# Fused double attention on one core: three maxima ahead of both score pairs in every step, two loads of A's keys moved, batch 0's maxima spread

## The reference

```python
# x: (8, 1024, 256) = (batch, token, channel)
xn = (x - mean) / sqrt(var + 1e-5)                  # over the channels
out = x + A(xn) + B(xn)

def A(h):       # latent attention: 8 heads, d_k 128, latent 32, rotary part 32
    c_q, c_kv = h @ W_DQ + b_DQ, h @ W_DKV + b_DKV  # 32 wide
    q = concat(c_q @ W_UQ + b_UQ, c_q @ W_QR + b_QR)            # 128 + 32 a head
    k = concat(c_kv @ W_UK + b_UK, h @ W_KR + b_KR)             # the 32 are shared
    v = c_kv @ W_UV + b_UV
    return softmax(q k^T / sqrt(160)) v, heads joined, @ W_O + b_O

def B(h):       # 16 heads of 16 dims, REG = 5 register tokens
    q, k, v = h @ W_qkv
    sim = mean over heads of cosine(q[5:], g_info), scaled to 0..1
    pos = sim > 0.9
    masked(m) = softmax(q k^T / 4 over registers and the tokens of m) v
    registers: (masked(pos) + masked(~pos)) / 2
    token: masked(pos) if pos[token] else masked(~pos)
    return all @ W_proj + b_proj
```

## Time and profile before

| | us |
|---|---|
| median of three runs | 2925.47 |
| lowest and highest | 2915.63, 2926.33 |
| the profiled execution, whole | 2916.49 |
| its span, from the first instruction to the last | 2914.7 |
| pass, in the profiled execution | 395.1 |
| A phases: batch 0, then the others | 127.8, 138.3 to 140.0 |
| B phases of batches 0 to 7 | 173.9, 180.2, 174.2, 178.7, 174.6, 177.8, 174.3, 160.3 |
| mean granted TensorE clock, 1 is full speed | 0.988 |

### The profile page before, as it was taken

One profiled execution on the slowest core, in us unless ns is written; L12 is line 12 of the kernel. 1 busy time (PEld: TensorE's weight loads), 2 busy tenths in 40 slices (PEclk: granted clock), 3 DMA queues, 4 the chain that ended last, 5 costly groups with the idle time before them and its releaser, 6 DMA issues.

```text
span 2914.7 us, 45214 instructions
## 1 busy us (share of the span) xinstructions
PE 2778.8 (95%) x16834; PEld 1264.0 (43%) x16834; DVE 2203.8 (76%) x4048; ACT 1761.9 (60%) x2143; POOL 1187.5 (41%) x424
## 2 busy tenths in 40 slices
PE   7899989999999999999999999999999999999997
PEld 5555534434443444444433444344434444344432
DVE  4566638788887788778878888878877887888880
ACT  3444445775467645775467646864577547754684
POOL 3323249214850088016721385118701672148411
PEclk9999989999999999999999999999999999999999
DMA  5855464234212520234122421352023412342001
GB/s 190 259 215 187 166 175 78 51 63 77 54 30 61 95 54 26 69 60 70 40 51 62 75 57 30 68 90 60 20 67 62 70 40 51 70 76 50 21 18 38
DMA packets 132636, 225.51 MB, mean 77 GB/s; under 512 B 52642, under 2 KB 83266, under 8 KB 130224
## 3 DMA queue, kind: packets, MB, share of 16 engines
q1 hardware_dynamic: 132416, 222.62, 31.4%
HBM read 143.70 MB, written 78.59 MB: 76 GB/s over the span
## 4 chain that ended last, share of the span: by engine, by line
PE 72%; DVE 21%; ACT 3%; issue 2%; DMA 1%; POOL 1%; SPq 0%; POOLq 0%; ACTq 0%; DVEq 0%
PE O L1266 21%; DVE mx L1538 17%; PE M L1178 15%; PE S L1248 7%; PE M L1172 7%; PE S L1245 7%; PE M L1224 2%; PE M L1132 2%; PE M L1226 2%; PE M L1215 2%; PE M L1150 1%; PE M L1191 1%; PE M L1146 1%; ACT PT L1019 1%; DVE QB L1519 1%
## 5 line engine op out<-in xcount | busy, mean ns | idle before, releaser
L1538 DVE TENSOR_REDUCE mx<-M 128x1 f32<-128x512 f32 x3037 | 1899.6, 681 | 389.4 <-PE M L1178 266.3
L1019 ACT ACTIVATE PTx<-S 128x1024 f32<-128x1024 f32 x768 | 744.4, 1022 | 461.3 <-PE S L1245 286.6
L1019 ACT ACTIVATE PT<-S 128x1024 f32<-128x1024 f32 x768 | 745.0, 1023 | 311.8 <-PE S L1245 151.1
L1178 PE MATMUL M<-KB,QB 50*128 50x512 f32 x2048 | 660.8, 479 | 33.5 <-DVE mx L1538 10.2
L889 POOL TENSOR_TENSOR SUM<-SUM,PTx 128x2048 f32<-128x2048 f32 x128 | 585.2, 4572 | 27.2 <-POOL SUM L889 22.2
L1178 PEld LDWEIGHTS M<-KB,QB 50*128 50x128 f32 x2048 | 278.8, 184 | 618.0 <-DVE mx L1538 316.5
L1248 PE MATMUL S<-QB,KB 52*128 52x512 f32 x2048 | 439.9, 427 | 4.0 <-ACT PT L1019 2.2
L1172 PE MATMUL M<-KA,QA 98*128 98x512 f32 x989 | 371.0, 446 | 14.6 <-DVE mx L1538 4.9
L889 POOL TENSOR_TENSOR SUM<-PT 128x2048 f32<-128x2048 f32 x64 | 292.2, 4566 | 170.7 <-ACT PT L1019 138.1
L1245 PE MATMUL S<-QA,KA 114*128 114x512 f32 (+1 forms) x1024 | 315.4, 417 | 9.6 <-ACT PT L1019 9.4
L1172 PEld LDWEIGHTS M<-KA,QA 98*128 98x128 f32 x989 | 169.5, 188 | 260.2 <-issue 120.3
(11 more groups left out here) (208 smaller groups left out, 1925.2 us busy)
## 6 DMA issues: line engine op xcount, KB each, us to landing
KA<-kt_d SPq DMA_DIRECT2D x48, 512.0 KB, 8.1
QB<-qk_d SPq DMA_DIRECT2D x192, 128.0 KB
KB<-qk_d SPq DMA_DIRECT2D x192, 128.0 KB
qk_d<-QB SPq DMA_DIRECT2D x16, 1024.0 KB, 4.2
kt_d<-QB SPq DMA_DIRECT2D x16, 1024.0 KB, 4.0
RB<-recb_d SPq DMA_DIRECT2D x64, 256.0 KB
vb_d<-VB SPq DMA_DIRECT2D x8, 1536.0 KB, 5.8
VB<-vb_d SPq DMA_DIRECT2D x8, 1536.0 KB, 9.3
```

Source lines behind the costliest of these rows:

```text
L1019: nc.scalar.activation(probs(k)[:, 2 * pair:2 * pair + 2, :], Sg[pair][:, :].rearrange("p (j s) -> p j s", j=2), ACT.Exp, scale=SCALE_A if ...
L1178: done = mm(m[:, :], QB[rows, 2 * q + a, at:at + P], KB[rows, 2 * q + a, keys], start=True, stop=True)
L1538: v.tensor_reduce(mx[:, g % 2, unit, kh:kh + 1], m[:, :], AX.X, ALU.max).then_inc(free, 1)
```

## The change

Four things change.

1. `jobs_b`: the units of every B step outside the registers' steps are laid out as (3, 0), all three ahead of the first pair, none between the pairs. Before it was (2, 1) for steps with B units; A units were (3, 0) already. A fourth unit stands behind the second pair as before.
2. `jobs_a`: the same for A steps with A units, 0 to 10, formerly (2, 1).
3. In the B phase the loads of A's keys move from steps 14 and 22 to steps 22 and 30. In the pass, the second half of batch 0's keys and its VA move out of "first" into a job "second" in batch 3.
4. Batch 0's B units, formerly at their common places in steps 10 to 31, are spread evenly over steps 6 to 31 by `first_slots`.

```diff
--- before.py
+++ after.py
@@ -39,7 +39,7 @@
 STORES = ("cq", "qk0", "kt0", "kb", "qk1", "kt1", "qk2", "qk3")
 RING = 4
 COS_PARTS = 8
-SILENT = ("x", "t", "ln", "root", "inv", "cq", "first", "cosroot", "cos", "draw")
+SILENT = ("x", "t", "ln", "root", "inv", "cq", "first", "cosroot", "cos", "draw", "second")
 PRIMED = 1
 RS_AT, RT_AT, RV_AT, RX_AT = 5, 11, 14, 19
 PO_B, PO_A = (45, 47, 53, 55), (13, 14, 15, 16)
@@ -67,7 +67,7 @@
     s += [("root", b + 1)] if more else [("cosroot", 6)]
     s += [("qk0", b, 0), ("qk0", b, 1), ("cq", b)]
     s += [("inv", b + 1)] if more else []
-    s += [("first",)] if b == 1 else []
+    s += [("first",)] if b == 1 else [("second",)] if b == 3 else []
     s += [("cosroot", b - 2)] if b in (2, 4, 6) else []
     s += [("kt0", b, 0), ("kt0", b, 1)] + (q[2:4] if more else []) + [("kb", b, 0), ("kb", b, 1)]
     s += [("va", b), ("qk1", b, 0), ("qk1", b, 1)]
@@ -134,6 +134,21 @@
 UNITS, FA = unit_slots()
 
 
+def first_slots(begin):
+
+    stream = [u for k in range(STEPS_A) for u in UNITS[k] if u[0] == "mb"]
+    units, ends, n = [[] for _ in range(STEPS_A)], [[] for _ in range(STEPS_A)], STEPS_A - begin
+    for i, u in enumerate(stream):
+        k = begin + i * n // len(stream)
+        units[k].append(u)
+        if i % (4 * NC) == 4 * NC - 1:
+            ends[k + 1].append(("fa", "b", u[1]))
+    return units, ends
+
+
+UNITS0, FA0 = first_slots(6)
+
+
 def lay(step, units, fa, sizes, behind):
 
     i, n = sizes[0], sizes[0] + sizes[1]
@@ -158,7 +173,7 @@
         units = [u for u in UNITS[STEPS_A + k] if more or u[0] == "mb"]
         fa = [j for j in FA[STEPS_A + k] if more or j[1] == "b"]
         registers = RV_AT <= k < RV_AT + NC // 2
-        sizes = (2, 0) if registers else (3, 0) if units and units[0][0] == "ma" else (2, 1)
+        sizes = (2, 0) if registers else (3, 0)
         lay(s[k], units, fa, sizes, registers)
     return s
 
@@ -172,9 +187,8 @@
         for c, at in enumerate(PO_A):
             s[at][2].append(("po", 4 + c))
     for k in range(STEPS_A):
-        units = [u for u in UNITS[k] if not first or u[0] == "mb"]
-        fa = [j for j in FA[k] if not first or j[1] == "b"]
-        sizes = (2, 1) if units and units[0][0] == "ma" else (2, 0) if k in PO_A else (3, 0)
+        units, fa = (UNITS0[k], FA0[k]) if first else (UNITS[k], FA[k])
+        sizes = (2, 0) if k in PO_A and not first else (3, 0)
         lay(s[k], units, fa, sizes, False)
     return s
 
@@ -694,11 +708,13 @@
                 wait_apart(sp, sel_in, 2 * HA * 16)
                 wait_apart(sp, zeros_in, 2 * 16)
                 wait_apart(sp, ones_out, 16)
-                for name in ("cq", "kt0", "kb", "kt1"):
+                for name in ("cq", "kt0", "kb"):
                     stored(0, name)
                 load_c(0)
                 load_a(0, 0)
                 load_kb(0)
+            elif kind == "second":
+                stored(0, "kt1")
                 load_a(0, 1)
                 wait_apart(sp, va_out[0], 16)
                 load_va(0)
@@ -738,9 +754,8 @@
 
         def a_steps(n, b, before):
             for k in range(STEPS_A):
-                for _, kind, g in FA[k]:
-                    if before or kind == "b":
-                        shift(n, kind, g, a_spot(n, b, ("fa", kind, g)))
+                for _, kind, g in FA[k] if before else FA0[k]:
+                    shift(n, kind, g, a_spot(n, b, ("fa", kind, g)))
                 if not before:
                     if k == 0:
                         for i in range(2):
@@ -802,9 +817,9 @@
                         load_c(n)
                         load_kb(n)
                         load_va(n)
-                    if k == 14:
+                    if k == 22:
                         load_a(n, 0)
-                    if k == 22:
+                    if k == 30:
                         load_a(n, 1)
                     if k > 5 * NC and k % NC == 2:
                         freed(b, k // NC - 5)
```

## The result

| | before | changed |
|---|---|---|
| median, us | 2923.01 (4 runs) | 2947.79 (4 runs) |
| lowest and highest | 2915.63, 2926.33 | 2945.22, 2952.33 |
| profiled execution: span | 2914.7 | 2944.4 |
| pass | 395.1 | 384.7 |
| A phase of batch 0 | 127.8 | 140.6 |

The ratio is 1.0095, with a 95% interval of 1.0074 to 1.0116: slower by about 25 us by the medians. The spans divide the difference of 29.7 us: the pass 10.4 shorter, batch 0's A phase 12.8 longer, the rest 27.3 longer. (The profiled execution of before was one of its faster ones, 2916.49, so the spans show some 5 us more than the medians.)

What follows compares the result with a forecast made beforehand. TensorE's order was taken as the bound, with the exponentials' loop equally long. The terms 36 - 14 - 10 - 4 gave +8 us, 2924.5; half the profiled run's distance to the median made it 2929 us, range 2890 to 2947.

Steps and rivals of the forecast that it cites:

- Part 1: B steps, three maxima ahead of the scores: first score pair and its exponential one slot later, +36 us over eight batches.
- The loop of 4.49 us for two steps: Plain B steps: the exponentials' loop has no slack, so two steps grow from 4.26 to 4.49 us.
- the bank's wait: Plain B steps: third maximum's PSUM bank comes 0.06 us after its place, so its weights load on arrival; 22 us more.
- The 2.65 us a batch of the plain steps: B steps 0 to 43: 23 steps with three maxima and no other delay lose 0.115 us each.
- rival two: Plain B steps: the third maximum's late bank adds to the exponentials' loop; 22 us more, 2951 us, chance 0.14.
- The even B stretches: B phases of even batches: to lengthen from 174.1 to near 178.5 us, by 4.5.
- The steps that wait for ScalarE: B steps 4, 10 to 13, 24, 34: score pair now behind the wait, one slot in six of seven, 1.4 us a batch.
- Part 2: A's first eleven steps, seven batches, three maxima ahead: cost nothing, hidden by VectorE's reductions; ends 18 us gained or lost.
- Part 3: B phase, A's key loads at steps 22 and 30: removes TensorE's stop at the registers' matmuls, 14 us gained.
- rival three: B phase: the stall follows the load to step 22, so no gain; +14, 2943 us, chance 0.12.
- Part 4: Pass, three key loads and VA's moved to batch 3: ScalarE's 8.10 us wait near 100 us goes, 10 us gained.
- Part 5: Batch 0's A phase, maxima over steps 6 to 31: steadier steps give back GpSimd's idle time, 4 us gained.

Runs made afterwards that it cites:

- e12: Changed kernel, but VectorE's reductions of B's maxima take 448 of the 512 keys: 2908.67 us, ratio 0.9952.
- e4: Changed kernel with only the B phase's loads of A's keys back at steps 14 and 22: 2964.73 us, ratio 1.0154.
- e10: Changed kernel with the pass as before, second run, timed beside e9: 2954.43 us, ratio 1.0113.
- e9: Changed kernel run again, unchanged: 2944.35 us, ratio 1.0079.
- e1: Changed kernel with only batch 0's B units back in steps 10 to 31: 2935.0 us, ratio 1.0048.
- e11: Changed kernel with B layout (2, 1), first B load ahead of the rows of ones, second after it lands, batch 0's units from step 10: 2895.19 us.
- e3: Changed kernel with only the B steps' layout back to (2, 1): 2907.8 us, ratio 0.9954.

## Why the prediction was wrong, point by point

**What bounds the kernel** was right: TensorE's order, with ScalarE's exponentials just beside it.

**Part 1 (said +36, measured about +39).** The loop of 4.49 us for two steps is there, to 0.01, once the bank's wait is taken out (e12). The 2.65 us a batch of the plain steps was somewhat low, as rival two said: the third maximum's bank is late in some plain steps as well, and 0.13 instead of 0.115 is lost in each. The even B stretches were forecast at 178.5 and are 178.8. The steps that wait for ScalarE were put at 1.4 us a batch; with both shortenings 2.0 are left.

**Part 2 (said 0).** The A phases of the later batches are 138.6 and were 138.3 to 138.4 when counted by the exponentials, and 138.4 in both when counted from O to O: no cost, as forecast. No run undoes this part alone, so that VectorE is what hides it is argued from the earlier trace rows and not shown.

**Part 3 (said -14).** By the spans -13; e4 gives 17 the other way. The stop didn't follow the loads to step 22: rival three is out. The reading as late code is borne out by the instruction packets of e4's section.

**Part 4 (said -10).** The pass is 10.4 shorter in the two profiled executions and 8.7 on average over all traces; e10 against e9 gives 10.1.

**Part 5 (said -4, bounds 0 and 8): the step that failed.** It measured +12.8 in the profiled pair, +8.0 by the changed kernel's second trace (135.8), and undoing it in e1 gave 9 to 13 back. The sentence was "Bounds: 0, as keys and queries of kind B arrive only about step 6": it took a late arrival as the end of the gain, not as a wait, and no row of a landing stands behind its step 6. In the kernel before the load was issued from 406.01, while step 4 ran, and landed at 425.5, between steps 8 and 9. A unit put ahead of that stands ahead of the scores on TensorE's own list, so all stops. The load is not sped up by an earlier use, and the stop is paid again in the clock: of the 12.1 us of steps 7 and 8 some 4 are that, against 3.4 and 4.6 at full clock. With the place and the load's order mended the same idea gave 7.5 us by the spans (127.8 to 120.3), near the upper bound said. Of these, 5.8 are steps 8 and 9 (e11); the rest is the load's order or the layout of steps 13 to 16.

**The sum.** 36 - 14 - 10 - 4 was +8. Measured by the spans: 40 - 13 - 10 + 13 = +30, the 40 being what is left for part 1; by the medians the whole is +25. Of the miss of 17 to 22, part 5 has 12 to 17 (said -4, measured +8 to +13), and part 1 3 to 4. The rival on the slow side named another mechanism, the bank's wait, and its size was far off (22 us said; its share here is a few us). No case held this one, and none of the rivals was of a load that isn't there yet.

## What to carry to other kernels

When work is moved earlier, find for each operand the row of its load's issue and of its landing in the trace of before; the first place where it can stand is the landing, and what stands behind it on the same engine waits with it. A stage whose step length is the same by two bounds at once has no slack, so that a slip of one slot in the order is paid in every second step; that can be worked out ahead from one timeline. To see what two overlapping waits cost, shorten both: either alone removes only a part.

## What was not expected of the hardware

The loads of B's keys and queries (128 KB transfers, 24 of them) kept the DMA engines at a share of 1.04 but moved 144 GB/s, and 194 in a second run of the same kernel, while the stores and loads near 100 us moved 369 at 0.93. A block of instructions that came 4 us later than usual, behind loads of 1.5 MB, stopped TensorE for 1.9 to 3.5 us. And a stop of TensorE costs more than its length: after the 16.5 us that ended at 420.5 the clock stayed at 0.50 until 434.1, and the two steps behind took 12.1 us instead of 8.0. In e3, after 12.2 us, it was back at 422.9, and the two took 8.6.
